# Attention and expert kernel: two of a batch's four scatters moved into the next step, drain bases put behind the scatters, first expert reordered, expert loop unrolled

## The reference

```python
x = x + xattn(layernorm(x), ctx, ctx, ...)      # keys and values: the 65 positions up to the query's own
y = layernorm(x)
probs = softmax(y @ router_w.T); k_probs, k_idx = top_k(probs, 2); k_probs /= k_probs.sum(-1)
rank = place of each (token, choice) among those of its expert; keep = rank < capacity
buf[e, rank] = y[token]                          # dispatch
h = silu(buf @ w1); out_buf = h @ w2             # 8 experts, 128 -> 512 -> 128
x = x + y + sum over the two choices of k_probs * out_buf[e, rank]
```

## Time and profile before

| | us |
|---|---|
| median of 3 runs | 547.12 |
| lowest and highest | 546.16, 550.73 |
| the profiled execution, as timed | 551.64 |
| its span in the trace | 549.6 |

### The profile page before, as it was taken

One profiled execution on the slowest core, in us unless ns is written; L12 is line 12 of the kernel. 1 busy time (PEld: TensorE's weight loads), 2 busy tenths in 40 slices (PEclk: granted clock), 3 DMA queues, 4 the chain that ended last, 5 costly groups with the idle time before them and its releaser, 6 DMA issues.

```text
span 549.6 us, 16557 instructions
## 1 busy us (share of the span) xinstructions
PE 420.5 (77%) x5590; PEld 324.7 (59%) x5590; DVE 344.3 (63%) x1055; ACT 262.0 (48%) x579; POOL 343.8 (63%) x289
## 2 busy tenths in 40 slices
PE   3463698789899999898988637699987977989300
PEld 2242476566777776676767523488866856767200
DVE  4784387877889888887887550366664655635200
ACT  1111255454556545564555520588865846657000
POOL 7442034467767777767565786038778787787774
PEclk9997799999999999997999967899988989789755
DMA  8996778488888887787684335436455454432332
GB/s 183 223 227 176 189 196 213 134 169 185 177 201 173 180 180 173 156 201 163 153 180 75 42 40 76 135 99 121 66 94 100 67 82 63 77 34 26 33 29 19
DMA packets 89183, 70.24 MB, mean 128 GB/s; under 512 B 9136, under 2 KB 75952, under 8 KB 88624
## 3 DMA queue, kind: packets, MB, share of 16 engines
q1 hardware_dynamic: 68144, 60.09, 42.4%
q0 software_dynamic: 20992, 9.53, 19.4%
HBM read 38.85 MB, written 30.74 MB: 127 GB/s over the span
## 4 chain that ended last, share of the span: by engine, by line
POOL 26%; issue 17%; DMA 7%; PE 5%; SPq 2%; DVE 1%; ACT 1%; POOLq 0%; DVEq 0%; ACTq 0%
POOL out L1349 18%; POOL queues L1273 6%; PE bank L457 4%; DMA out<-ys,row_token 3%; DMA k_scratch<-parts 2%; DMA k_pack<-k_scratch 1%; SPq L340 1%; POOL base L1305 1%; DMA queues<-rows,index 1%; DMA xs<-queues 0%; SPq L345 0%; POOL parts L1325 0%; POOL rest L1322 0%; DVE xTp L1153 0%; PE bank L681 0%
## 5 line engine op out<-in xcount | busy, mean ns | idle before, releaser
L1349 POOL DMA_INDIRECT out<-ys,row_token x88 | 138.4, 1573 | 63.5 <-DVE ys L1206 27.1
L892 DVE TENSOR_REDUCE maxima<-bank 128x4 f32<-128x512 f32 x128 | 87.2, 685 | 49.1 <-PE bank L457 46.9
L1273 POOL DMA_INDIRECT queues<-rows,index x64 | 100.5, 1571 | 19.7 <-issue 19.7
L758 ACT ACTIVATE probs<-bank 128x512 f32<-128x512 f32 x128 | 76.4, 597 | 68.7 <-PE bank L457 67.1
L457 PE MATMUL bank<-xTp,w1p 128*128 128x512 f32 (+1 forms) x288 | 71.4, 403 | 12.4 <-DVE xTp L1153 12.3
L457 PE MATMUL bank<-k_pack,q_pack 128*64 128x128 bf16 x1024 | 55.6, 235 | 20.1 <-DMA k_pack<-k_scratch 19.1
L457 PEld LDWEIGHTS bank<-xTp,w1p 128*128 128x128 f32 x288 | 53.6, 212 | 24.6 <-issue 8.2
L863 ACT ACTIVATE hid<-bank 128x512 f32<-128x512 f32 (+1 forms) x96 | 53.6, 558 | 26.3 <-PE bank L457 25.6
L457 PE MATMUL bank<-q_pack,k_pack 128*128 128x64 bf16 x1024 | 54.1, 197 | 12.9 <-DMA q_pack<-maxT 11.3
L1231 DVE TENSOR_TENSOR hidp<-hid,hidp 128x512 fp32r<-128x512 f32 (+1 forms) x96 | 55.5, 601 | 12.6 <-ACT hidp L867 10.5
L457 PE MATMUL bank<-hidp,w2p 128*128 128x512 f32 (+1 forms) x288 | 62.8, 368 | 0.5 <-DVE hidp L1231 0.5
(11 more groups left out here) (116 smaller groups left out, 680.2 us busy)
## 6 DMA issues: line engine op xcount, KB each, us to landing
k_pack<-k_scratch SPq DMA_DIRECT2D x64, 192.0 KB, 4.0
q_pack<-q_scratch SPq DMA_DIRECT2D x64, 128.0 KB, 3.2
queues<-empty SPq DMA_DIRECT2D x8, 682.5 KB, 7.6
xs<-queues SPq DMA_DIRECT2D x7, 650.0 KB
q_scratch<-parts SPq DMA_DIRECT2D x16, 192.0 KB
k_scratch<-parts SPq DMA_DIRECT2D x16, 192.0 KB
xin<-in_x SPq DMA_DIRECT2D x16, 128.0 KB, 3.0
cin<-in_ctx SPq DMA_DIRECT2D x16, 128.0 KB, 3.5
```

Of the source, the lines that this page charges most:

```text
L758: nc.scalar.activation(probs[u % 2][:], bb[u % 2][:], ACT.Exp).then_inc(S["prob_s"], 1)
L892: v.reduce_max(maxima[par][:, 4 * hg:4 * hg + 4, i2], ab[u % 2][:].rearrange("p (h c) -> p h c", c=P), AX).then_inc(S["max_s"], 1)
L1273: g.indirect_dma_start(queues, bass.IndirectOffsetOnAxis(ap=index[par][:, n:n + 1], axis=0), rows[par][:, n // TILES, n % TILES, :], None, ...
L1349: g.indirect_dma_start(out, bass.IndirectOffsetOnAxis(ap=row_token[par][0:n, t:t + 1], axis=0), ys[s][0:n, col // P, :], None, compute_op= ...
```

## The change

It has four parts.

1. **Scatters.** `rows_out` is split in `rows_ready` (the waits) and `row_out` (one indirect DMA). For batches 0 to 10 the first two of the four DMAs stay at the end of step k, and the other two go out in the next step: one ahead of `qk`, one between `qk` and `rest`.
2. **Drain bases.** In steps 14 to 17 `base` stands behind the four scatters instead of ahead of `rstd2`.
3. **First expert.** PE's order for expert 0 is written out: `out_of_hidden` of a chunk stands right behind its `hidden`, and the results of chunks 0 and 1 are transposed one chunk sooner. DVE's tags, and ACT's copies, move to match.
4. **Loops.** Steps 2 and 3 are written out (`LOOP` 2 to 4), and all eight experts are.

```diff
-        FIRST, LOOP, END, LAST = -4, 2, 10, 18
+        FIRST, LOOP, END, LAST = -4, 4, 10, 18
+        DRAIN = BATCHES - 3
...
         def experts(eng, body):
-            body(0, 0)
-            with eng.Fori(0, (EX_END - EX_LOOP) // 2) as n:
...
+            for e in range(EXPERTS):
+                body(e, e % 2)
@@ tensor
+            def first_expert():
+
+                hidden(0, 0, 0, 0)
+                rows_across(0, 0, 1)
+                out_of_hidden(0, 0, 0, 0)
+                hidden(0, 0, 1, 1)
+                results_across(0, 0, 0)
+                rows_across(0, 0, 2)
+                out_of_hidden(0, 0, 1, 1)
+                hidden(0, 0, 2, 0)
+                results_across(0, 1, 1)
+                rows_across(1, 1, 0)
...
-                    elif not first:
+                    elif e > 1 or c == 1:
                         results_across(e - 1, c + 1, s)
@@ scalar
-                    if c >= 1:
+                    if first and c == 0:
+                        split_weights(e + 1, 1 - par)
+                    if first and c < 2:
+                        copy_results(e, c, s)
+                    elif not first and c >= 1:
                         copy_results(e, c - 1, 1 - s)
@@ vector
-                        if f == 3 and first and c == 2:
-                            weigh_results(e, par, 0, s)
+                        if f == 0 and first and c >= 1:
+                            weigh_results(e, par, c - 1, 1 - s)
...
-                    elif not first:
+                    elif e > 1 or (e == 1 and c == 1):
                         weigh_results(e - 1, 1 - par, c + 1, s)
+                    if c == (0 if first else 1):
+                        tags(e, par)
@@ gpsimd
             def body(k, par, pair):
+                last_steps = isinstance(k, int) and k > DRAIN
...
+                    if not last_steps:
+                        base_of_output()
+                    token_numbers()
...
+                late = not isinstance(k, int) or k <= DRAIN
+                if late:
+                    row_out(k - 3, 1 - par, 2)
                 if on(k + 3):
...
                     g.tensor_tensor(qk[:], straight[:], turned[:], ALU.add).then_inc(S["qk_s"], 1)
+                if late:
+                    row_out(k - 3, 1 - par, 3)
+                if on(k + 3):
...
-                rows_out(k, par)
+                rows_ready(k - 2, par)
+                for n in range(2 if not isinstance(k, int) or k < DRAIN else 2 * TILES):
+                    row_out(k - 2, par, n)
+                if last_steps and on(k - 2):
+                    base_of_output()
```

More of the change, by code:

```diff
@@ L398, in body @@
                 pack(k + 2, par, 2)
[L399 removed]
+                if isinstance(k, int) and -2 <= k < 2:
                     empty_queues(*REST_OF_QUEUES[k + 2])
@@ L717, in body2 @@
                     hidden(e, par, c, s)
-                    if first and c == 2:
-                        results_across(e, 0, s)
                     if c < NCH - 1:
@@ L725, in body2 @@
                         out_of_hidden(e, par, c - 1, 1 - s)
-                    elif not first:
+                    else:
                         out_of_hidden(e - 1, 1 - par, NCH - 1, 1 - s)
-                    if c >= 2 and not first:
+                    if c >= 2:
                         results_across(e, c - 2, s)
-                    elif not first:
+                    elif e > 1 or c == 1:
                         results_across(e - 1, c + 1, s)
@@ L872, in body2 @@
                         copy_results(e - 1, NCH - 1, 1 - s)
-                    if c == 0:
+                    if c == 0 and not first:
                         split_weights(e + 1, 1 - par)
@@ L1271, in rows_out, with row_out @@
                 apart(pool, "past_pool")
[L1272 to L1275 removed]
+            def row_out(j, par, n):
+                if not on(j):
+                    return
+                g.indirect_dma_start(queues, bass.IndirectOffsetOnAxis(ap=index[par][:, n:n + 1], axis=0),
+                                     rows[par][:, n // TILES, n % TILES, :], None, compute_op=ALU.add
+                                     ).then_inc(S[f"scattered{par}"], 16)
             def start():
```

30 lines of the change are left out of this document (10 added, 20 removed).

## The result

| | us |
|---|---|
| before, median beside it (lowest, highest) | 546.64 (545.91, 550.73) |
| after, median of 4 (lowest, highest) | 565.64 (560.29, 569.47) |
| ratio, with 95% interval | 1.0327 (1.0279 to 1.0375) |
| profiled execution of after, as timed; its span | 569.47; 567.6 |

The change makes the kernel 3.3% slower; between the medians it is 19.0 us, where 8.1 was forecast, and the time lies just above the range. The ratio is that of the fast executions alone (17.9 us) and leaves out the profiled one, which lies 1.6% above the fastest. A second measurement gave 1.0335 (1.0284 to 1.0387), and its profile has the same gaps in the drain (10.97 and 6.20 us where this one has 11.09 and 6.21).

What follows compares the result with a forecast made beforehand. The prediction took POOL, with a DVE answer, to set the loop's pace and POOL's chain the drain's. Terms -6.6 + 8.1 + 4.2 - 0.7 + 1.5 + 1.6 gave +8.1 on the 547.12 median: 555.2 us, range 545 to 565.

Steps and rivals of the forecast that it cites:

- a): Step loop: two scatters issued a step later shorten eight steps from 16.63 to 15.8 us each, -6.6 us.
- g): Written-out loops: gaps ahead of scatters stay as they are, 0 us.
- b): Drain, step 14 (E: its last scatter's end): base behind scatters holds SP's queue, delaying the next scatters, +8.1 us.
- e): Weights of expert 0, behind the last `out<-base` in SP's queue, go out later and delay the first `hidden`, +1.5 us.
- d): Drain, steps 16 and 17: no `xres` behind; in step 17 `base` no longer stands ahead of the scatters, -0.7 us.
- f): First expert: chunk 0's results come 4.0 us sooner, but waits ahead of the third chunk use that up, +1.6 us.
- Rival 4: Loop: no gain, since `parts` goes out later through scratch memory to PE; 561.8 us, chance 0.18.
- c): Drain, step 15: `xres` held behind the base's transfer, so the next scatters start at E+5.96, +4.2 us.

Runs made afterwards that it cites:

- one_late: The kernel before with one scatter of the four, the fourth, issued a step later, ahead of `qk`; ratio to before 0.9982 (0.9953 to 1.0011).
- loop_at_4: The kernel before with steps 2 and 3 written out and nothing else changed; ratio to before 1.0007 (0.9972 to 1.0041).
- only_unrolled: The kernel before with its loops written out (steps 2 and 3, all eight experts) and nothing else changed; ratio to before 1.0067 (1.0030 to 1.0104).
- no_drain_bases: The changed kernel with `base` of steps 14 to 17 back ahead of `rstd2`; ratio to the kernel before 1.0040 (0.9998 to 1.0082).
- only_bases: The kernel before with only the drain bases moved behind the scatters; ratio to before 1.0329 (1.0259 to 1.0400).
- only_first: The kernel before with the first expert's new order and the loops written out; ratio to before 1.0131 (1.0046 to 1.0215).

## Why the prediction was wrong in size

The direction, and the part that carries it, were right; the sum is short by 10.9 us between the medians. By the sizes below, two terms make most of it: the gain of a) did not come (6.6), and the nothing of g) was some 3.7. Then b) and e) were short by 1.0 each, and the 0.7 of d) was no gain. The range was also narrower than its parts: the upper bounds of a) to f) add up to 568, and it ended at 565.

- **a) Late scatters, -6.6: wrong in what the loop gains.** The step that failed is "the waits that PE keeps are those for maxima and packed inputs, so I take 15.8". Regular steps are at 15.6 to 16.2 (mean of steps 6 to 10), but those waits do not stay as they were. They grow in the loop's first turn, to two steps of together 34.7 to 37.1 us in all nine profiles with late scatters and the loop at 4, in seven of them with the clock at 0.50 for a part. Ten steps take what they take without late scatters. Rival 4, no gain in the loop, held; its reason (`parts` goes out later) is not all of it, since one_late had the long steps too. The 16.63 of the baseline was high as well: 16.4 in loop_at_4.
- **b) Step 14, +8.1: right in every link, wrong in its start.** The gap was 11.1 where E+10.9, and +1.0 for the clock, was forecast. PE's idle time was 7.83 ("about 7"). The low clock (0.50 in the window below) cost next to nothing, and not the +1.0: `x1` came at E+8.45 for E+8.3. But the E+3.78 that I subtracted belongs to one execution. With the bases ahead, the gap was 1.93 to 1.96 in ten other profiles, so the edit costs 9.1. The same long gap is part of why that execution lay 4.5 above the median; I took the 4.5 off the sum and left the long gap in the baseline. (The 2.3 us by the Trainium skill, DMA: Bandwidth & Descriptors, Anatomy of one DMA, is that page's fit for transfers that GpSimd issues; these are SP's, and the row's 2.0 stands.)

```profile
309.00:313.00 4.00, 0.00 (x0) 0.00 (x0) 0.00 (x0) 0.00 (x0) 1.18 (x3) 0.50 0.46 84
313.00:317.00 4.00, 3.77 (x65) 3.26 (x66) 1.09 (x7) 2.35 (x6) 0.00 (x0) 0.50 0.02 4
```

- **c) Step 15, +4.2: right.** E+6.2 for E+5.96, 4.4 more.
- **d) Steps 16 and 17, -0.7: a miscount.** The gap ahead of step 17's scatters is 2.48 for 2.52. The base of step 17 has gone from it, but that of step 16, now behind its own scatters, stands there in its place. POOL of the changed kernel, behind the last scatter of step 16:

```profile
340.48 1.25 POOL L1324 TENSOR_TENSOR base<-x,rows 128x256 f32<-128x256 f32 x1
...
343.49 1.57 POOL L1289 DMA_INDIRECT queues<-rows,index  x1 [1.61 <-issue]
```

- **e) Weights, +1.5: the wrong link.** ACT's first cast came at E+5.0, as forecast, but `hidden` at E+9.3 and not E+8.2 (E+8.4 to E+9.6 in five profiles with the bases behind, E+6.5 to E+6.8 in nearly all others). It waits for the rows' load, which stands behind the weights in SP's queue: issued at E+2.3 for E+2.0, it took 4.4 us to land where it took 2.7 before, beside the 512 KB of weights, and PE's transposes took 1.11 for 0.66, at a granted clock of 0.50 for 1.00: 0.35 + 1.7 + 0.45 = 2.5. The forecast had this only as its upper bound (weights and rows arrive together). DMA issues, 340 to 362, and PE's transposes, each before and now:

```profile
xs<-queues SPq DMA_DIRECT2D x1, 260.0 KB, 2.7
```

```profile
xs<-queues SPq DMA_DIRECT2D x1, 260.0 KB, 4.4
```

```profile
345.58 0.66 PE L681 MATMUL bank<-cst,xs 128*128 128x128 f32 x4 [1.94 <-DMA xs<-queues]
```

```profile
357.39 1.11 PE L677 MATMUL bank<-cst,xs 128*128 128x128 f32 x4 [4.32 <-DMA xs<-queues]
359.91 4.37 PE L453 MATMUL bank<-xTp,w1p 128*128 128x512 f32 x12 [1.40 <-DVE xTp L1166]
```

- **f) First expert, +1.6: right.** -4.1 and +5.2, with PE's waits as forecast. The +5.2 is the same within 0.1 in all seven profiles with the new order; the -4.1 lay between -5.4 and -2.6.
- **g) Written-out loops, 0: wrong.** The evidence was scatters within a row (0.30). The cost is ahead of an expert's first scatter, +4.2 in the trace and 0.7% in only_unrolled; the gaps grow where code is loaded and where weights go out beside the last scatter.

With the measured sizes the sum against a typical execution is 0 (a) + 9.1 + 4.4 + 2.5 + 1.1 + 3.7 (0.67% of 546) = 20.8, beside the 17.9 to 19.0 found. The agreement does not prove each small term: the last two give 4.8, and no_drain_bases, which has them and the late scatters, is 2.2 us slower than before (at most 4.5 by its interval).

## What to carry to other kernels

A queue that waits at its head for a result delays everything behind it: here moving a 0.72 us operation behind four scatters cost 17 us (only_bases), since operands of the next step stood behind its transfer. Its other readers and overwriters count too: with the queue cleared, the next result still waited for the moved operation to free its buffer. A baseline gap read from one profiled execution has to be compared with others before it is subtracted, above all where that execution lies above the median. Where an operation moves behind a step's work, the next step's gap gets it: in step 17 nothing was gained. Of a loop the total counts, first turn included, and not its regular step.

## What the runs showed that I had not expected

- A stall of PE of 2.17 us in the loop went with 10.2 us at the low clock, and the step became 21.6 us long in place of 15 to 16. One of 2.85 us in only_first did not: its clock stayed at 1.00.
- With late scatters the first turn of the step loop took 34.7 to 37.1 us for two steps, where later ones took 30.5 to 33; it moved with the loop's start.
- With 512 KB of weights issued 0.5 to 0.7 us behind its start, an indirect scatter landed after 3.5 to 3.6 us in place of 2.5 to 2.9, and after 4.4 to 4.9 where a load of code came too.
- Written-out experts load code in two queues, 16 KB at a time in one of them; where such a load fell 1.5 to 2.2 us behind the start of the last scatter ahead of expert 6, the gap grew from 2.1 to between 3.05 and 3.95 us.
